# A two-expert-layer macaron block on one core: shorter moments, a 65th weight column, a later GpSimd subtraction, and idle-time products on TensorE

## What is computed

```python
x = x + 0.5 * ffn(layernorm(x), router_w, w1, v1, w2)
x = x + attention(layernorm(x), Wq, bq, Wk, bk, Wv, bv, Wo, bo)
x = x + 0.5 * ffn(layernorm(x), router_w, w1, v1, w2)
```

```python
logits = x @ router_w.T                       # 64 experts
probs = softmax(logits); wts, idx = top_k(probs, 8)
wts = wts / sum(wts)
# each expert takes its first 32 tokens (C = 32), in order of tokens
h = silu(xg @ w1.T) * (xg @ v1.T);  y = h @ w2   # F = 96
out[token] += y * weight of the pair
```

## Time and profile before

| | |
|---|---|
| Three runs | 709.76, 708.3, 709.78; median 709.76 |
| The profiled execution | 710.26, its span 708.4 |
| TensorE busy | 622.9 (88%), 4530 instructions |
| VectorE busy | 509.8 (72%), 1289 instructions |
| ScalarE busy | 374.4 (53%) |
| GpSimd busy | 53.8 (8%), 57 instructions |
| Mean granted TensorE clock | 0.949 |

### The profile page before, as it was taken

How to read it: one execution, slowest core, us unless ns; L and a number is a source line. 1 busy time by engine, 2 the same in 40 slices (tenths; PEclk the granted TensorE clock), 3 DMA queues, 4 the chain that set the end, 5 groups by cost and what they waited for, 6 DMA issues and landing times.

```text
span 708.4 us, 12001 instructions
## 1 busy us (share of the span) xinstructions
PE 622.9 (88%) x4530; PEld 529.1 (75%) x4530; DVE 509.8 (72%) x1289; ACT 374.4 (53%) x1013; POOL 53.8 (8%) x57
## 2 busy tenths in 40 slices
PE   1729988899999999999999999999999998644995
PEld 1406667699988979999897999898799997422774
DVE  6665536688997777778777777876878776893442
ACT  1504534576756655656555656565566565421441
POOL 3153200000000000000000000000000000133310
PEclk9859989999999999999999999999999999875998
DMA  9949960000000000000000000000000042794571
GB/s 329 407 166 393 420 183 2 1 1 1 0 1 2 1 1 1 1 1 1 1 0 1 1 1 1 1 1 1 1 1 1 1 187 111 281 403 124 196 253 47
DMA packets 27133, 62.50 MB, mean 88 GB/s; under 512 B 6880, under 2 KB 17120, under 8 KB 26816
## 3 DMA queue, kind: packets, MB, share of 16 engines
q1 hardware_dynamic: 25008, 55.92, 21.0%
q0 software_dynamic: 1632, 5.38, 2.2%
q10 hardware_dynamic: 432, 0.39, 0.2%
HBM read 54.34 MB, written 7.34 MB: 87 GB/s over the span
## 4 chain that ended last, share of the span: by engine, by line
PE 77%; DVE 12%; DMA 5%; ACT 4%; issue 2%; SPq 0%; POOL 0%; DVEq 0%
PE bank L1214 18%; PE bank L1216 18%; PE bank L1215 18%; PE bank L1266 8%; PE bank L1056 3%; PE bank L1095 3%; DMA down_r<-down_in 3%; PE bank L1105 2%; PE bank L1027 1%; DVE best L789 1%; DVE ln L709 1%; PE bank L1040 1%; DVE keys L791 1%; PE bank L1139 1%; DMA x<-x_in 1%
## 5 line engine op out<-in xcount | busy, mean ns | idle before, releaser
L624 ACT ACTIVATE probs<-bank,negmax 128x256 f32<-128x256 f32 x256 | 121.4, 494 | 0.3 <-DVE negmax L939 0.3
L637 ACT CAST probsT_hi<-bank 128x512 fp32r<-128x512 f32 x128 | 68.9, 590 | 81.0 <-PE bank L1266 81.0
L971 DVE TENSOR_TENSOR probsT_lo<-bank,probsT_hi 128x512 fp32r<-128x512 f32 x128 | 82.0, 683 | 1.4 <-ACT probsT_hi L637 1.4
L939 DVE TENSOR_REDUCE negmax<-bank 128x2 f32<-128x512 f32 x128 | 82.0, 681 | 1.1 <-PE bank L1216 1.1
L607 ACT ACTIVATE o_hi<-bank,bv 128x512 fp32r<-128x512 f32 x64 | 44.2, 690 | 64.9 <-PE bank L1216 64.9
L1214 PE MATMUL bank<-k_hi,q_hi 128*128 128x256 f32 x256 | 72.6, 283 | 2.9 <-DVE q_lo L925 2.9
L947 DVE TENSOR_SCALAR probs<-probs,rowinv 128x256 f32<-128x256 f32 x256 | 73.1, 350 | 2.3
L1214 PE MATMUL bank<-o_hi,wo_hi 128*128 128x256 f32 x256 | 73.1, 286 | 1.6 <-DVE o_lo L925 1.6
L925 DVE SCALAR_TENSOR_TENSOR o_lo<-bank,bv,o_hi 128x512 fp32r<-128x512 f32 x64 | 48.0, 751 | 36.3 <-ACT o_hi L607 36.3
L1216 PE MATMUL bank<-o_hi,wo_lo 128*128 128x256 f32 x256 | 72.5, 283 | 0.0
L1216 PE MATMUL bank<-k_hi,q_lo 128*128 128x256 f32 x256 | 72.5, 283 | 0.0
(11 more groups left out here) (165 smaller groups left out, 1318.1 us busy)
## 6 DMA issues: line engine op xcount, KB each, us to landing
up_r<-up_in SPq DMA_DIRECT2D x16, 768.0 KB, 9.3
down_r<-down_in SPq DMA_DIRECT2D x14, 512.0 KB, 10.1
up_q<-up_in SPq DMA_DIRECT2D x8, 768.0 KB, 8.2
up_o<-up_in SPq DMA_DIRECT2D x6, 768.0 KB, 11.9
down_q<-down_in SPq DMA_DIRECT2D x8, 512.0 KB, 9.0
token_table<-xn SPq DMA_DIRECT2D x16, 256.0 KB, 10.0
down_o<-down_in SPq DMA_DIRECT2D x6, 512.0 KB, 13.6
x<-x_in SPq DMA_DIRECT2D x4, 512.0 KB, 5.5
```

What stands on the lines that cost most here:

```text
L624: nc.scalar.activation(probs[:, n % 2, t, :], scores_ps[head][:, qt * S:qt * S + S], ACT.Exp, bias=negmax[:, n % 2, t:t + 1], accum_out=ro ...
L637: nc.scalar.copy(probsT[0][:, head].rearrange("p c s -> p (c s)"), probsT_ps[head][:]).then_inc(probsT_high, 1)
L939: nc.vector.reduce_max(negmax[:, n % 2, 2 * head:2 * head + 2], scores_ps[head][:].rearrange("p (t s) -> p t s", t=2), AX.X, negate=True). ...
L971: nc.vector.tensor_tensor(probsT[1][:, head].rearrange("p c s -> p (c s)"), probsT_ps[head][:], probsT[0][:, head].rearrange("p c s -> p ( ...
```

## The change

- **Moments.** The expression is rewritten with a constant KEPT = 0.375 folded into the variance, and the three equal Newton rounds become one round of four instructions with other constants and one of three. There are 4 + 4 + 3 = 11 levels, and the second level has two instructions in place of three.
- **Weights.** GpSimd no longer multiplies by the reciprocal sum. VectorE writes half the reciprocal into a 65th column of expw; a row of the table is 321 values (1,284 bytes) in place of 320 (1,280 bytes). The slot's weight product becomes one SCALAR_TENSOR_TENSOR that also multiplies by that column. `store_weights` waits for both.
- **GpSimd's subtraction** waits for the last mask as well.
- **Unread products**: 24 at the very start of TensorE's program, behind the wait for the constants; `keep_busy(16)` between the product that gives the slots and the wait for the first gather, in both layers; `keep_busy(12)` ahead of layer 1.

```diff
-ROW = D + E
+ROW = D + E + 1
+KEPT = 0.375
-                expw = sb(router, "expw", [P, TILES, E])
+                expw = sb(router, "expw", [P, TILES, E + 1])
             def store_weights():
                 sp.wait_ge(weights_ready, weights_seen.add())
+                sp.wait_ge(winv_ready, inv_seen.add())
                 pool.wait_ge(top8_ready, tops.add(4))
-                nc.gpsimd.tensor_tensor(expw[:], logits[:], top8[:, :, 0:1].to_broadcast([P, TILES, E]),
+                pool.wait_ge(chosen_ready, masks.add(4))
+                nc.gpsimd.tensor_tensor(expw[:, :, 0:E], logits[:], top8[:, :, 0:1].to_broadcast([P, TILES, E]),
                                         ALU.subtract).then_inc(shifted, 1)
                 pool.wait_ge(exps, exp_seen.add(2))
-                pool.wait_ge(winv_ready, inv.add())
-                nc.gpsimd.tensor_tensor(expw[:], expw[:], wsum[:, 1, :].unsqueeze(2).to_broadcast([P, TILES, E]),
-                                        ALU.mult).then_inc(scaled_ready, 1)
-                pool.wait_ge(chosen_ready, masks.add(4))
-                pool.wait_ge(scaled_ready, scales.add())
...
-                          (tt, var, stats[:, a:b, 2], stats[:, a:b, 5], ALU.add)],
-                         [(stt, gap2, half_gap, 0.25, half_gap, ALU.mult, ALU.mult), (ts, var, var, 1.0 / D, EPS, ALU.mult, ALU.add),
-                          (ts, mean_, mean_, 0.5, None, ALU.mult)],
-                         [(tt, var, var, gap2, ALU.add)],
+                          (stt, var, stats[:, a:b, 2], EPS * D, stats[:, a:b, 5], ALU.add, ALU.add)],
+                         [(stt, gap2, half_gap, 0.25 / KEPT ** 2, half_gap, ALU.mult, ALU.mult), (ts, mean_, mean_, 0.5, None, ALU.mult)],
+                         [(stt, var, var, 1.0 / D / KEPT ** 2, gap2, ALU.mult, ALU.add)],
...
                 steps += [[(tt, gap2, rstd_, rstd_, ALU.mult)],
-                          [(stt, gap2, gap2, -0.5, var, ALU.mult, ALU.mult)],
-                          [(stt, rstd_, gap2, 1.5, rstd_, ALU.add, ALU.mult)]] * 3
+                          [(tt, gap2, gap2, var, ALU.mult)],
+                          [(stt, gap2, gap2, -10.0 / 3.0, gap2, ALU.add, ALU.mult)],
+                          [(stt, rstd_, gap2, 5.0, rstd_, ALU.add, ALU.mult)]]
+                steps += [[(tt, gap2, rstd_, rstd_, ALU.mult)],
+                          [(stt, gap2, gap2, -0.5 * KEPT ** 2, var, ALU.mult, ALU.mult)],
+                          [(stt, rstd_, gap2, 1.5, rstd_, ALU.add, ALU.mult)]]
...
-                    tie(nc.vector.tensor_tensor(weight4[:, parity, :], slots[:, u, s + D:ROW:GROUPS], quadrant[:], ALU.mult))
+                    tie(nc.vector.scalar_tensor_tensor(weight4[:, parity, :], slots[:, u, s + D:D + E:GROUPS], slots[:, u, D + E:ROW],
+                                                       quadrant[:], ALU.mult, ALU.mult))
...
-                        nc.vector.tensor_scalar(wsum[:, 1, :], wsum[:, 1, :], 0.5, None, ALU.mult).then_inc(winv_ready, 1)
+                        nc.vector.tensor_scalar(expw[:, :, E], wsum[:, 1, :], 0.5, None, ALU.mult).then_inc(winv_ready, 1)
...
                 last.then_inc(slot_raw, 1)
+                keep_busy(16)
                 transpose_slots(0, 0)
...
             pe.wait_ge(constants, 2)
+            for _ in range(24):
+                mm(bank[3][:, 0:P], ident[:], ident[:], start=True, stop=True)
             pe.wait_ge(small_loaded, 80)
             expert_layer(0)
...
             output()
+            keep_busy(12)
             expert_layer(1)
```

More of the change, by code:

```diff
@@ L217, in macaron_kernel @@
         chosen_ready = sem("chosen_ready")
-        scaled_ready = sem("scaled_ready")
         shifted8 = sem("shifted8")
@@ L351, in _ @@
                 sp.dma_start(dst[:], src).then_inc(small_loaded, 16)
-            xn_seen, weights_seen = Tally(xn_ready), Tally(weights_ready)
+            xn_seen, weights_seen, inv_seen = Tally(xn_ready), Tally(weights_ready), Tally(winv_ready)
             def load(layer, g):
@@ L447, in _ @@
             raw, tops, exp_seen = Tally(key_raw), Tally(top8_ready), Tally(exps)
-            scales = Tally(scaled_ready)
-            masks, inv, slot_seen = Tally(chosen_ready), Tally(winv_ready), Tally(slot_ready)
+            masks, slot_seen = Tally(chosen_ready), Tally(slot_ready)
             written = Tally(table_written)
@@ L463, in expert_layer @@
                 pool.wait_ge(top8_ready, tops.add(4))
-                nc.gpsimd.tensor_tensor(expw[:], logits[:], top8[:, :, 0:1].to_broadcast([P, TILES, E]),
+                pool.wait_ge(chosen_ready, masks.add(4))
+                nc.gpsimd.tensor_tensor(expw[:, :, 0:E], logits[:], top8[:, :, 0:1].to_broadcast([P, TILES, E]),
                                         ALU.subtract).then_inc(shifted, 1)
                 pool.wait_ge(exps, exp_seen.add(2))
-                pool.wait_ge(winv_ready, inv.add())
-                nc.gpsimd.tensor_tensor(expw[:], expw[:], wsum[:, 1, :].unsqueeze(2).to_broadcast([P, TILES, E]),
-                                        ALU.mult).then_inc(scaled_ready, 1)
-                pool.wait_ge(chosen_ready, masks.add(4))
-                pool.wait_ge(scaled_ready, scales.add())
                 nc.gpsimd.tensor_tensor(
-                    expw[:].rearrange("p (h i) e -> p h i e", h=2), expw[:].rearrange("p (h i) e -> p h i e", h=2),
+                    expw[:, :, 0:E].rearrange("p (h i) e -> p h i e", h=2), expw[:, :, 0:E].rearrange("p (h i) e -> p h i e", h=2),
                     chosen[:].rearrange("p i h e -> p h i e"), ALU.mult).then_inc(weights_ready, 1)
@@ L562, in expert_layer @@
                 act.wait_ge(shifted, shift_seen.add())
-                nc.scalar.activation(expw[:], expw[:], ACT.Exp).then_inc(exps, 1)
+                nc.scalar.activation(expw[:, :, 0:E], expw[:, :, 0:E], ACT.Exp).then_inc(exps, 1)
                 warm(ACT.Silu)
```

## The result

The changed kernel takes **716.89 us** (median of 4 runs, 713.49 to 717.47) against 709.03 for the kernel before in the same comparison (4 runs, 707.47 to 709.78): ratio 1.0121, 95% interval 1.0085 to 1.0157. It is slower by 7.9, and lies outside the predicted range. The profiled execution took 717.47, its span is 715.7 (before 708.4), its mean granted clock 0.961.

What follows compares the result with a forecast made beforehand. Layer 0 was taken as bound by a string of waits, then DMA loads; layer 1's first gather by the table. Terms -0.5 - 0.4 - 0.8 + 0.4 + 0.3 = -1.0 took 709.76 to 708.8 us; range 705.8 to 711.2.

Steps and rivals of the forecast that it cites:

- The moments: Start of layer 0, on VectorE: two levels and one instruction fewer, -0.5 us on the path.
- The mask: Layer 0's last mask: with GpSimd's subtraction behind it, it takes 0.29 in place of 1.12, -0.8 us.
- The column's instruction: Layer 0, L797's successor on VectorE: held until GpSimd's mask product ends, 0 to +0.4 us, taken as +0.4.
- The 24 products: TensorE's start in layer 0: a higher clock for transposes and router products, -0.4 us, between nothing and 1.5 gained.
- The 16 products in layer 1: Ahead of layer 1's first gather: TensorE idles again about 2 us behind them, so first groups gain 0.
- The rival that the clock holds: Clock stays up behind the 24 and 16 products: 1.1 more in transposes, 1.9 in layer 1, 705.8 us; chance 0.34.
- The table: Layer 1's stores before the first gather: weights issued 0.3 earlier, uneven row starts cost some; taken +0.3, -0.3 to +1.9.
- the table is ready before slot_index in layer 0 either way: Layer 0: dropping GpSimd's multiplication by wsum (1.90) brings no gain, since the table is not what the gather awaits.
- the loads behind it: Layer 0 from the gather on: bound by DMA loads, so an earlier gather moves the whole rest of layer 0.
- TensorE's branch: Behind layer 0, at 107.3: takes 3.73, to 111.0, and covers the moments there, whose two levels cost nothing.
- The rival "the table is late": Layer 1: uneven starts slow stores and gathers; 710.4 at a fifth less rate, 712.9 at 1.6 times the time; chance 0.18.
- What counts in layer 1: Layer 1 up to the gather: slot_index comes 0.9 earlier but waits 3.9 for the table, worth 0.

Runs made afterwards that it cites:

- experiment 1: The kernel before with table rows of 321 values, the 65th column an unread zero, and nothing else of the change: 720.61 us, ratio 1.0206.
- experiment 6: experiment 4 with GpSimd's subtraction ahead of the last mask again: 704.85 us, ratio 0.9968 against the kernel before.
- experiment 7: experiment 4 with layer 1's token stores ahead of loads 8 to 11 and the weights' store ahead of 10 and 11: 702.99 us, ratio 0.9937.
- experiment 4: The changed kernel without the 65th column: rows of 320 values, GpSimd multiplies by the reciprocal sum again: 706.04 us, ratio 0.9978 against the kernel before.
- experiment 5: experiment 4 without the 24, 16 and 12 unread products: 704.93 us, ratio 0.9964 against the kernel before.
- experiment 11: experiment 7 with loads 10 and 11 behind a wait for the first three gathers: 701.72 us, ratio 0.9925 against the kernel before.
- experiment 12: experiment 7 with GpSimd's subtraction ahead of the last mask again: 704.06 us, ratio 0.9954 against the kernel before.
- experiment 2: The changed kernel with table rows of 336 values (1,344 bytes), the last 15 zeros: 708.38 us, ratio 1.0020 against the kernel before.
- experiment 3: The changed kernel with table rows of 328 values (1,312 bytes): 710.47 us, ratio 1.0070 against the kernel before.
- experiment 10: The changed kernel, rows of 321 values, with the store order of experiment 7 in layer 1: 715.14 us, ratio 1.0100 against the kernel before.

## Why the prediction was wrong

**The moments, right in length, and not seen on the path.** They are 0.5 shorter (2.59 against 3.09). In this profile they also began 0.5 later, VectorE having waited 0.53 for a piece of x, so the first `xn` came no earlier. Of the ten other versions with the shorter moments, six had no such wait, and their first `xn` is at 13.5 to 13.6; with it and the old moments (experiment 1) it is at 14.3. That wait is scatter, and the term is worth its 0.5 against an execution with the same wait. **The mask, right:** 1.12 became 0.29, in both layers. **The column's instruction, right in kind:** it is held until GpSimd's product ends. I took +0.4; in layer 0 it is 0.17, in layer 1 0.31 (0.48 long), and 0.84 with rows of 336. The rows show an instruction with gaps in its destination ending 0.04 behind GpSimd's product. The Trainium skill, "VectorE: DVE Perf Modes", section "What auto-detection actually checks", gives the two-port mode to one source with source and destination in SBUF, if their outermost dimensions are even or equal, and names no stride; 16 is even, and the rows agree with it. First `xn` to slot_index lost 0.78, as the rows add up (-0.83 for the mask, +0.17 for the column, -0.1 for the products); the moments are not in that stretch.

**The 24 products, a size off.** I took -0.4. They took 8.06, between 5.6 and 11.1 as expected. The transposes fell from 2.94 to 2.51, but the router products behind them rose from 1.46 to 1.78, so 0.1 is left: the clock fell at 15.4 and rose at 18.9. The 16 products in layer 1 gained nothing, as the forecast took: the rise was at 643.5 and the fall at 650.3, before the late gather even began. The rival that the clock holds did not come about in this kernel where it counts; in experiments 6 and 7, where data came sooner behind the products, it did.

**The table, the step that failed.** Two sentences of it were wrong. The first is the term +0.3 in layer 1, whose upper end I drew at +1.9 from a fifth less rate, reasoning that the token rows would fall at worst to the rate of 256-byte rows. From the first load to the gather it is 42.85 where it was 37.13: **+5.7**. The rates fell by three tenths in the token rows and by half to two thirds in the weights, and 256-byte rows are no floor, since the rows of weights lose their even starts as well. The second is "the table is ready before slot_index in layer 0 either way". Before, the weights were ready at 41.6 and the table still came in time for slot_index; in the change they are ready 5.4 sooner and the wait is 5.2, since slow token stores and the loads behind them are ahead of them in the DMA engines. The gather came 4.2 later, and the loads behind it moved with it, as the prediction had it: the longest one ended at 101.28 in place of 95.63, 5.6 later. That attention began only 1.9 later is no work of these loads: TensorE waited no less for them (4.6 against 4.0). From that load's end to attention it took 15.1 in place of 18.8, for two reasons that the prediction did not have. In the kernel before, the clock was at its lower level there from 97.2 to 104.0 and again from 110.8 to 114.2, and in the change it was not; that is as much luck as gain. And TensorE's branch, which the prediction took at 3.73, is short in both layers of the change, where 1.08 of it stood in the chain before:

```profile
L1184 PEldq COMPARE_BRANCH  x2: 318/344/371, 110.5 to 707.6; - x2
```

The longer of its two executions took 3.3 to 3.8 in the five versions without the added unread products and under 0.5 in the nine with them. Experiments 4 and 5, which differ in nothing else, have 0.46 and 3.65, so the products shorten it. No experiment took them out one by one, so which of them does it, and why, stays open. TensorE then waited 1.3 for VectorE's `xn` behind layer 0, where the prediction counted VectorE's work as covered. Together, 1.9 + 5.7 less the attention's 0.3 is the span's 7.3.

The rival "the table is late" was the right mechanism with the right place in layer 1, undersized at 1.6 times the stores' time (+4.4), and not drawn for layer 0. Of its two parts only the stores slowed; the gathers did not (2.93 against 2.94). The beats that the Trainium skill counts ("DMA: Bandwidth & Descriptors", section "How a descriptor splits into AXI transactions"), up to 40 in place of 32, point the right way and give an estimated quarter more time for a row at most; experiment 1 shows 379 falling to between 269 and 246 GB/s, four to five tenths more. Nor do they set the widths apart as measured: by them a row takes an estimated 38 beats at most with 336 and 39 with 328, and those cost a fraction. The measurement decides.

**What counts in layer 1, right.** A sooner slot_index was worth nothing there, as the forecast said: experiment 4 has it 1.8 sooner and the gather no sooner; only experiments that took the table out of the way had use for it.

Two things stay open. Experiment 1, with the wide rows alone, is 6 slower than the whole change by the ratios; the two profiled executions are only 2.2 apart (717.9 and 715.7), 1.3 of it at the first gather in layer 0, and I found no row for the rest. And why a store is slow at such starts can't be told from these views. For the token rows only the place in HBM changed; for the weights' rows also their length and their place in SBUF.

## What to carry to other kernels

Before a row of a table in HBM gets one more word, work out where each row then starts. Here multiples of 1,280 bytes kept the full rate, 1,344 and 1,312 lost 8 to 18% of it in the token rows, and 1,284 lost three tenths there and more in the short rows. Put the extra value elsewhere, or measure a padded row (here GpSimd's multiplication by the sum, which cost nothing on the path, did as well or better). A cost that no row of the profile shows deserves a wide bound, not one taken from the nearest pleasant row: the bytes per row said "hardly changes", and the start of the row decided. When an engine's work is shortened, look for the wait that ends last at the same place; here it was the table in layer 1, and only a queue reordered for it let the router's gain through. And when an unread product is meant to hold the clock, look at how long TensorE stands still behind it, not at the products alone.

## What the runs showed of the hardware

- Stores of 1 KB rows at starts of multiples of 1,284 bytes ran at 246 to 274 GB/s at the end of layer 1's token stores, and at 220 in layer 0; at 1,280 at 378 to 379 in the matching stretches. Multiples of 1,344 gave 324 to 348, of 1,312 311 to 330.
- Rows of 260 bytes at starts of multiples of 1,284 ran at 86 to 166 GB/s, rows of 256 at 1,280 at 271 to 298, of 320 at 1,344 at 244, of 288 at 1,312 at 216. The DMA share stood over 1 in all of these stretches, so a full share is no sign of a full rate.
- The gathers, which read rows of 1,284 bytes out of the same table, took as long as before (2.93 against 2.94).
- A VectorE instruction of 128x16 with gaps in its destination took 0.34, 0.48 and 1.01 beside a GpSimd product, each time ending 0.04 behind it. The same instruction without gaps took 0.17 with GpSimd idle; the one with gaps never ran beside an idle GpSimd.
- The granted clock rose 2.8 to 4.4 us into the 16 unread products of layer 1, in all nine profiles that have them. It stayed up where TensorE then stood still for 1.4 to 1.6 at most (experiments 6, 7, 11, 12), and fell where it stood still for 2.6 or more (the change, experiments 2, 3, 4, 10).
- The longer execution of TensorE's branch took 3.3 to 3.8 in the five profiles without the added unread products and 0.36 to 0.46 in the nine with them; the cause was not sought.
